# The last unit of a convolution-attention kernel: softmax in two column parities, six PSUM banks, a fused gelu, and idle matmuls

## The chip, the cores and the metric

The kernel runs on one core of one Trainium2 chip. The metric is the device time of one execution in microseconds (us); lower is better. TensorE (PE) does the matmuls and can write only to PSUM, VectorE (DVE) and ScalarE (ACT) work element by element and read PSUM and SBUF, GpSimd (POOL) adds in SBUF, SyncE (SP) issues the loads and stores.

## The reference

`x` is 4 x 256 x 64 x 64 in float32. Two layers follow each other:

```
k    = conv7x7(x, w1, dilation 2) + b1 ; k = conv1x1(k, w2) + b2      # 49 logits a pixel
attn = softmax(k, axis=1)                                             # over the 49 taps
y    = sum over taps (u,v) of attn[u,v] * x shifted by (2u, 2v)       # 256 channels
g    = gelu(yc[c, column] + y * D[c]);  o = y + g                     # yc from a small linear scan
out  = layer_norm over the 256 channels of o, times ln_w, plus ln_b
```

## The kernel before, in words

Dilation 2 lets even and odd image rows be treated apart, so the work is cut into 8 **units** (4 images x 2 row parities), each of 32 rows x 64 columns x 256 channels. Each unit passes through these stages: the convolution on PE (`conv`, into the four PSUM banks of `cv`); the logits `Z`, with a column parity `w` (even or odd columns) as an index; the softmax; the spreading of the attention into banded matrices; the application of the bands to the turned input `XT`; gelu and residual; and the layer norm. A software pipeline written out by hand, one instruction list per engine, does the convolution of unit n while the later stages of unit n-1 run on the other engines and in gaps of PE. The order of each list is the order of execution on its engine; semaphores (`wait_ge`) join the lists.

After the convolution of the last unit nothing is left to overlap with. The functions `unit(...)` end, and a tail for unit `m = 7` is written out on each engine:

- **Softmax.** PE turns the logits of one column parity into the two banks of `wk` (`turn_logits`, L457), DVE sums the taps into `E` (`gather_taps`, L1208 and L1210), and only then may PE turn the other parity into the same banks. DVE takes the maximum over the 49 taps (L1216), ACT does 16 exponentials of 128 x 49 (L737), DVE divides (L1222 to L1226), ACT rounds the result to fp16 (`attention_high`, L742), DVE makes the remainder (`attention_low`, L1230). All of these but the turning and the gathering work on both parities at once, 128 x 784 elements. PE turns the attention into `ms` (`turn_attention`, L467) and ACT copies it to `AT` (L746).
- **Spread.** Ten rows r: PE does 32 small matmuls into `wk[:, r % 2]` (`spread`, L478), ACT copies the bank to `band` in fp16 (`band_high`, L751), DVE makes the remainder (`band_low`, L1235). Row r waits for `band_low` of row r-2.
- **Application.** Eight pieces y: half of the rows q, half of the channels h, column parity w. PE does 15 matmuls into `wk[:, y % 2]` (`apply`, L495). ACT scales the bank into `o` (`attended`, L760). For each pair of column parities DVE makes the argument of gelu (`gelu_args`, L1250), ACT applies gelu (L766), DVE adds (`residual`, L1256).
- **Layer norm of the last unit in quarters.** POOL sums the halves (L408), PE makes the mean (`last_mean`, L669), DVE centres (L1571), ACT squares (L982), PE makes the variance into `cv` (`last_variance`, L677), ACT loads another table of functions (L1010) and makes the inverse deviation (L987, L989), DVE normalises (L1579), and the quarters are stored.

Unit 6 still owes parts of its own layer norm at that point: `variance` (L516), `inverse_deviation` (L781, L783), two `normalise` on DVE (L1269), two `scale_shift` on ACT (L787) and two stores behind them.

## Time and profile before

| | us |
|---|---|
| median of 3 runs | 895.67 (894.84 to 896.17) |
| profiled execution | 896.21 |
| its span | 894.4 |
| PE busy | 803.0 (90%) |
| DVE busy | 722.4 (81%) |
| ACT busy | 519.9 (58%) |
| POOL busy | 188.4 (21%) |

The span runs from the first to the last recorded event of the profiled execution. Positions below are in us from its start. "Busy" counts compute instructions only. A matmul's record is pipelined with its neighbours, so that the start of the next instruction tells more than the length of one. The granted clock of TensorE is given as a share of its 2.4 GHz level: 1.00 is 2.4 GHz and 0.50 is 1.2 GHz.

### The profile page before, as it was taken

The page shows a single profiled execution, that of the slowest core. Times are in us where ns is not written, and L with a number is a line of the kernel's source. Part 1 is how long each engine was busy: PE and PEld are TensorE (multiplying, and loading weights), DVE is VectorE, ACT ScalarE, POOL GpSimd, SP SyncE. Part 2 cuts the span into 40 slices and gives each one's busy share as a digit, 9 for nine tenths or more (in the row PEclk, how much of TensorE's full clock was granted, in tenths as well). Part 3 has the DMA queues.
Part 4 walks back from the last instruction along what each step waited for, and adds up shares of the span by engine and source line. Part 5 has one row for each costly group of instructions (what it writes and reads, how often), then busy time and mean ns, then how long its engine had stood idle before and what let it go on. Part 6 is the DMA issues. An engine that isn't in the chain of part 4 may idle for free.

```text
span 894.4 us, 27128 instructions
## 1 busy us (share of the span) xinstructions
PE 803.0 (90%) x12261; PEld 493.8 (55%) x12261; DVE 722.4 (81%) x876; ACT 519.9 (58%) x834; POOL 188.4 (21%) x100
## 2 busy tenths in 40 slices
PE   4979787999997999899997999899989999996485
PEld 4975333575555655565564645565546655663451
DVE  3899769889995999689986999599967999677336
ACT  2363232766674666665584767557665659465546
POOL 3114102112510233013311151024301341021010
PEclk9999889999997999999997999999997999999588
DMA  9322005000125010700151011601070011002103
GB/s 312 72 52 45 2 2 95 2 3 2 48 53 92 3 48 2 143 3 1 49 113 33 2 48 42 104 1 40 11 143 2 1 49 50 3 1 64 32 1 94
DMA packets 133597, 41.78 MB, mean 47 GB/s; under 512 B 133145, under 2 KB 133226, under 8 KB 133226
## 3 DMA queue, kind: packets, MB, share of 16 engines
q1 hardware_dynamic: 132248, 40.01, 19.9%
q8 instruction: 96, 1.57, 0.7%
q10 hardware_dynamic: 1234, 0.04, 0.1%
q14 instruction: 19, 0.16, 0.1%
HBM read 23.27 MB, written 16.78 MB: 45 GB/s over the span
## 4 chain that ended last, share of the span: by engine, by line
PE 51%; DVE 15%; issue 12%; ACT 11%; DMA 8%; POOL 1%; SPq 1%; DVEq 0%; ACTq 0%; POOLq 0%
PE cv L438 26%; DMA raw<-in_x_dram 7%; PE wk L495 6%; PE pcomp L603 5%; PE wk L478 4%; PE ms L516 3%; ACT chs L737 3%; ACT V L700 3%; PE wk L529 2%; DVE R L1028 2%; DVE tg L1250 2%; PE wk L457 2%; DVE V L1110 1%; DVE XT L1139 1%; DVE Z L1158 1%
## 5 line engine op out<-in xcount | busy, mean ns | idle before, releaser
L438 PE MATMUL cv<-V,W 128*32 128x496 f16 (+6 forms) x7840 | 447.1, 383 | 19.7 <-issue 7.5
L438 PEld LDWEIGHTS cv<-V,W 128*32 128x32 f16 (+1 forms) x7840 | 201.5, 97 | 224.7 <-issue 41.6
L313 POOL TENSOR_TENSOR R<-raw 128x1152 f32<-128x1152 f32 x32 | 100.2, 3130 | 258.4 <-DVE V L1110 93.8
L700 ACT ACTIVATE V<-R,sc 128x1024 f16<-128x1024 f32 (+1 forms) x88 | 110.5, 1274 | 55.1 <-PE cv L438 54.3
L1110 DVE SCALAR_TENSOR_TENSOR V<-R,sc,V 128x1024 f16<-128x1024 f32 (+1 forms) x88 | 122.4, 1399 | 9.7 <-ACT V L700 9.6
L478 PE MATMUL wk<-AT,sel 128*128 128x16 f16 x2560 | 85.1, 192 | 23.1 <-DVE band L1235 21.2
L495 PE MATMUL wk<-band,XT 128*128 128x224 f16 (+1 forms) x960 | 102.9, 268 | 2.6 <-DVE band L1235 1.4
L478 PEld LDWEIGHTS wk<-AT,sel 128*128 128x128 f16 x2560 | 79.6, 103 | 44.7 <-DVE band L1235 29.6
L495 PEld LDWEIGHTS wk<-band,XT 128*128 128x128 f16 x960 | 83.3, 99 | 25.5 <-issue 5.3
L1235 DVE TENSOR_TENSOR band<-wk,band 128x512 f16<-128x512 f32 x80 | 54.7, 689 | 44.0 <-ACT band L751 43.8
L751 ACT CAST band<-wk 128x512 f16<-128x512 f32 x80 | 46.7, 584 | 69.4 <-PE wk L478 68.4
L731 ACT ACTIVATE XT<-wk,sc 128x512 f16<-128x512 f32 x64 | 42.9, 681 | 53.6 <-PE wk L529 52.9
L760 ACT ACTIVATE o<-wk,sc 128x512 f32<-128x512 f32 x64 | 45.7, 730 | 46.7 <-PE wk L495 46.6
L1041 DVE SCALAR_TENSOR_TENSOR R<-R 128x1024 f32<-128x1024 f32 (+1 forms) x56 | 72.5, 1298 | 0.2
L1028 DVE SCALAR_TENSOR_TENSOR R<-raw 128x512 f32<-128x512 f32 (+1 forms) x48 | 48.2, 1047 | 27.5 <-DMA raw<-in_x_dram 27.4
L1139 DVE SCALAR_TENSOR_TENSOR XT<-wk,sc,XT 128x512 f16<-128x512 f32 x64 | 47.2, 746 | 16.5 <-ACT XT L731 16.3
L338 POOL TENSOR_TENSOR chs<-o 128x1024 f32<-128x1024 f32 x14 | 36.7, 2622 | 110.4 <-DVE o L1256 95.1
L344 POOL TENSOR_TENSOR chs<-tg 128x1024 f32<-128x1024 f32 x14 | 34.5, 2462 | 96.3 <-ACT tg L773 96.3
L603 PE MATMUL pcomp<-w2t,w1raw 128*128 128x48 f32 x196 | 45.0, 418 | 9.4 <-DMA w1raw<-in_L_conv_w_dram 9.4
L1250 DVE SCALAR_TENSOR_TENSOR tg<-o,dcol,yc 128x1024 f32<-128x1024 f32 x32 | 40.4, 1279 | 13.4 <-ACT o L760 13.1
L529 PEld LDWEIGHTS wk<-id,raw 128*128 128x128 f32 x256 | 35.1, 208 | 27.9 <-issue 14.2
L603 PEld LDWEIGHTS pcomp<-w2t,w1raw 128*128 128x128 f32 x196 | 43.7, 312 | 10.0 <-issue 9.6
(138 smaller groups left out, 903.1 us busy)
## 6 DMA issues: line engine op xcount, KB each, us to landing
raw<-in_x_dram SPq DMA_DIRECT2D x16, 1024.0 KB, 11.5
out_dram<-o SPq DMA_DIRECT2D x28, 512.0 KB, 3.9
w1raw<-in_L_conv_w_dram SPq DMA_DIRECT2D x2, 3136.0 KB, 16.8
out_dram<-o SPq DMA_DIRECT2D x8, 256.0 KB, 3.4
cm<-in_L_conv_Cmat_dram ACTq DMA_DIRECT2D x1, 32.0 KB, 8.4
dcol<-in_L_conv_D_dram ACTq DMA_DIRECT2D x2, 0.5 KB, 9.8
lnw<-in_L_conv_ln_w_dram ACTq DMA_DIRECT2D x2, 0.5 KB, 7.2
lnb<-in_L_conv_ln_b_dram ACTq DMA_DIRECT2D x2, 0.5 KB, 7.2
```

What stands on the lines that cost most here:

```text
L313: nc.gpsimd.tensor_tensor(R[buffer][:, :, :, :], rows_of(par, j + 2), rows_of(par, j), ALU.subtract).then_inc(pool_rows, 1)
L438: ins = pe.matmul(to.rearrange("p (w t c) -> p w t c", w=2, c=COLS)[:, :, :, c0:c1], W[:, ws, h * K7 + v, k0:k1], slot(n, a)[:, low, :, t0 ...
L478: ins = pe.matmul(wk[:, r % 2, c * TILES:(c + 1) * TILES].rearrange("p (w j) -> p w j", w=2), sel[:, s, f:f + P], AT[:, :, r:r + 29:4, c], ...
L495: ins = pe.matmul(wk[:, y % 2, (r0 - 16 * q) * COLS:(r1 - 16 * q) * COLS], XT[:, xl, 8 * w + j, h, :], band[:, bl, 8 * w + j, r0 - 4 * j + ...
L603: last = pe.matmul(pcomp[:, g % 3, v * P:v * P + REL], w1h[:, u * K7 + v, :], w2t[:, 0:REL], start=True, stop=True)
L700: nc.scalar.activation(v_array(n, a, 0), array(a), ACT.Identity, scale=sc[:, par, 3:4]).then_inc(vhi, 1)
L1028: nc.vector.scalar_tensor_tensor(out=R[buffer][:, 0:wins, h, :], in0=raw[par][:, h, r:r + 4 * wins - 3:4, :], scalar=-4.0, in1=raw[par][:, ...
L1041: nc.vector.scalar_tensor_tensor(out=part(*out), in0=part(*a), scalar=factor, in1=part(*b), op0=ALU.mult, op1=ALU.add).then_inc(row_made, 1)
L1110: nc.vector.scalar_tensor_tensor(out=v_flat(n, a, 1), in0=array_flat(a), scalar=sc[:, par, 3:4], in1=v_flat(n, a, 0), op0=ALU.mult, op1=AL ...
L1139: nc.vector.scalar_tensor_tensor(out=low, in0=wk[:, g % 2, :], scalar=sc[:, par, 3:4], in1=high, op0=ALU.mult, op1=ALU.subtract).then_inc( ...
L1235: nc.vector.tensor_tensor(band[:, 1, :, r, :], wk[:, r % 2, :].rearrange("p (c t) -> p t c", t=TILES), band[:, 0, :, r, :], ALU.subtract). ...
L1250: nc.vector.scalar_tensor_tensor(out=tg[:, h], in0=o[:, q, h], scalar=dcol[:, h:h + 1], in1=yc[:, h].unsqueeze(1).broadcast_to([P, 16, WID ...
```

## The change

Only the last unit's tail is changed, on all engines but SP.

1. **Softmax per column parity.** The logits of parity 0 are turned into `wk`, those of parity 1 into `cv[:, 0:2]`, without a wait between them. Sums, maximum, exponentials, division, rounding and turning back are done for each parity by itself (128 x 392 elements); the attention is turned into `cv` banks 2 and 3 instead of `ms`.
2. **Unit 6's remainders** move: the first `normalise` goes behind the division of parity 0, the second behind the attention's remainder of parity 1; the two `scale_shift` go between `band_high` of rows 1 and 2 and of rows 3 and 4.
3. **Idle matmuls.** `keep_running` puts 22 and then 9 matmuls of 128 x 480, whose results nobody reads, on PE into `wk` bank 0 while the softmax runs.
4. **Six banks.** `spread` and `apply` of the last unit rotate over `wk` and `cv` (6 banks) instead of `wk` alone (2). The variances of the last layer norm go to `var_bank`, all four of `cv`.
5. **Gelu and sum straight from PSUM.** `attended` is dropped. For each piece y, DVE makes the argument from PSUM (`last_args`), ACT applies gelu to 128 x 512 (`last_gelu`), and DVE reads PSUM again for the sum (`last_residual`). A column `ds` = `dcol` times the scale is made once.

The core of the diff:

```diff
+IDLE_MATMULS = (22, 9)
+        last_banks = [wk[:, 0, :], wk[:, 1, :]] + [cv[:, i, :] for i in range(4)]
+        spread_bank = lambda m, r: last_banks[r % 6] if m == LAST else wk[:, r % 2, :]
+        apply_bank = lambda m, y: last_banks[(0, 1, 4, 5, 2, 3, 0, 1)[y]] if m == LAST else wk[:, y % 2, :]
...
-                if r >= 2:
-                    pe.wait_ge(blo, 10 * m + r - 1)
+                banks = 6 if m == LAST else 2
+                if r >= banks:
+                    pe.wait_ge(blo, 10 * m + r - banks + 1)
...
+                if m == LAST and y >= 6:
+                    pe.wait_ge(l_res, y - 5)
+                if m < LAST and y >= 2:
                     pe.wait_ge(xs_made, 8 * m + y - 1)
...
+            def keep_running(w):
+                if w == 0:
+                    pe.wait_ge(l_soft, 2)
+                for _ in range(IDLE_MATMULS[w]):
+                    pe.matmul(wk[:, 0, 0:5 * 2 * REL], id16[:, :], W[:, 0, 0:5, :].rearrange("p s k -> p (s k)"),
+                              start=True, stop=True)
...
-            turn_logits(m, 0)
-            turn_logits(m, 1)
-            turn_attention(m, 0)
-            turn_attention(m, 1)
+            last_logits(0)
+            last_logits(1)
+            keep_running(0)
+            last_attention(0)
+            keep_running(1)
+            last_attention(1)
...
-            for i in range(2):
-                pool.wait_ge(o_made, 4 * (UNITS - 1) + 2)
+                pool.wait_ge(l_res, 4)
...
+            for y in range(7):
+                last_gelu(y)
             last_squares(0)
-            gelu(m, 1, 1)
+            last_gelu(7)
...
+                nc.vector.scalar_tensor_tensor(out=tg[:, h, :, w:WIDTH:2],
+                                               in0=apply_bank(m, y).rearrange("p (r c) -> p r c", c=COLS),
+                                               scalar=ds[:, h:h + 1],
+                                               in1=yc[:, h, w:WIDTH:2].unsqueeze(1).broadcast_to([P, 16, COLS]),
+                                               op0=ALU.mult, op1=ALU.add).then_inc(l_args, 1)
...
+                nc.vector.scalar_tensor_tensor(out=o[:, q, h, :, w:WIDTH:2],
+                                               in0=apply_bank(m, y).rearrange("p (r c) -> p r c", c=COLS),
+                                               scalar=scale_of_last, in1=tg[:, h, :, w:WIDTH:2],
+                                               op0=ALU.mult, op1=ALU.add).then_inc(l_res, 1)
```

How the instructions now stand. TensorE behind the last variance of unit 6, before; `wk<-id,Z` turns logits, `ms<-id,HL` turns the attention, and in the list after this one `wk<-AT,sel` is a matmul of a spread row:

```order
L457 MATMUL wk<-id,Z 128x128 [waits x_turned_low,logit_steps]
L457 MATMUL wk<-id,Z 128x128 x7
L457 MATMUL wk<-id,Z 128x128 [waits softmax_steps]
L457 MATMUL wk<-id,Z 128x128 x7
L467 MATMUL ms<-id,HL 128x128 [waits normed,softmax_steps]
L467 MATMUL ms<-id,HL 128x128 x7
```

The same place in the changed kernel:

```order
L677 MATMUL wk<-id,Z 128x128 [waits x_turned_low,logit_steps]
L677 MATMUL wk<-id,Z 128x128 x7
L677 MATMUL cv<-id,Z 128x128 x8
L686 MATMUL wk<-W,id 128x480 [waits last_softmax_steps]
L686 MATMUL wk<-W,id 128x480 x21
L692 MATMUL cv<-id,HL 128x128 [waits last_softmax_steps]
L692 MATMUL cv<-id,HL 128x128 x7
L686 MATMUL wk<-W,id 128x480 x9
L692 MATMUL cv<-id,HL 128x128 [waits last_softmax_steps]
L692 MATMUL cv<-id,HL 128x128 x7
L492 MATMUL wk<-AT,sel 128x16 [waits att_copied]
L492 MATMUL wk<-AT,sel 128x16 x63
```

The second turning has lost its wait, the turning back is in two parts, and the 22 and 9 idle matmuls stand in PE's list ahead of one part each. ScalarE over the softmax and the spread in the changed kernel (before, the two `o<-o,lnb,lnw` stood ahead of 16 exponentials in a row, one cast, two copies to `AT` and ten `band` casts):

```order
L1017 ACTIVATE chs,st<-chs,st 128x49 x3
L1022 CAST HL<-chs 128x8x49 [waits last_softmax_steps]
L1017 ACTIVATE chs,st<-chs,st 128x49 [waits last_softmax_steps]
L1017 ACTIVATE chs,st<-chs,st 128x49 x3
L1026 COPY AT<-cv 128x1024 [waits att_turned]
L1022 CAST HL<-chs 128x8x49 [waits last_softmax_steps]
L1026 COPY AT<-cv 128x1024 [waits att_turned]
L795 CAST band<-wk 128x16x32 [waits band_spread] x2
L831 ACTIVATE o<-o,lnb,lnw 128x1024 [waits normed]
L795 CAST band<-cv 128x16x32 [waits band_spread] x2
L831 ACTIVATE o<-o,lnb,lnw 128x1024 [waits normed]
```

VectorE at the end of the application in the changed kernel, where `tg<-` is `last_args`, `o<-...,tg` is `last_residual` and `o<-o,ms` is a half of a centring:

```order
L1696 SCALAR_TENSOR_TENSOR tg<-wk,ds,yc 128x512 [waits y_done,last_residual]
L1708 SCALAR_TENSOR_TENSOR o<-cv,sc,tg 128x512 [waits last_gelu]
L1673 TENSOR_TENSOR o<-o,ms 128x512 [waits last_residual,q_mean,q_sum]
L1673 TENSOR_TENSOR o<-o,ms 128x512
L1696 SCALAR_TENSOR_TENSOR tg<-wk,ds,yc 128x512 [waits y_done,last_residual]
L1708 SCALAR_TENSOR_TENSOR o<-wk,sc,tg 128x512 [waits last_gelu]
```

Each piece now has one pair of DVE instructions of 512 elements a partition; before, a pair of pieces had two of 1024, behind two copies on ACT.

## Rows read from the trace of the kernel before

**Rows 1.** The page's costly groups (count, busy us, mean ns, idle) and its DMA issues.

```profile
L751 ACT CAST band<-wk 128x512 f16<-128x512 f32 x80 | 46.7, 584 | 69.4 <-PE wk L478 68.4
...
out_dram<-o SPq DMA_DIRECT2D x28, 512.0 KB, 3.9
```

**Rows 2.** Windows of the tail: busy us (instructions) by engine, PEclk, DMA share, GB/s.

```profile
820.00:824.00 4.00, 1.89 (x16) 1.42 (x14) 3.17 (x4) 2.68 (x3) 0.00 (x0) 0.96 0.00 0
840.00:844.00 4.00, 3.12 (x98) 2.90 (x95) 2.10 (x4) 2.20 (x4) 0.00 (x0) 0.50 0.00 0
857.00:858.00 1.00, 1.00 (x8) 0.70 (x7) 0.00 (x0) 0.00 (x0) 0.00 (x0) 0.58 0.00 0
860.00:864.00 4.00, 3.21 (x35) 2.64 (x33) 1.68 (x3) 2.60 (x5) 0.00 (x0) 1.00 0.02 4
```

**Rows 3.** Timeline of TensorE: start, us, line, tiles, count [idle before, releaser].

```profile
797.08 3.36 PE L438 MATMUL cv<-V,W 128*32 128x480 f16 x60
...
822.18 1.09 PE L457 MATMUL wk<-id,Z 128*128 128x128 f32 x8 [1.38 <-DVE chs L1210]
835.63 1.89 PE L467 MATMUL ms<-id,HL 128*128 128x128 f16 x16 [12.36 <-DVE HL L1230]
838.68 2.10 PE L478 MATMUL wk<-AT,sel 128*128 128x16 f16 x64 [1.17 <-ACT AT L746]
...
852.36 8.89 PE L495 MATMUL wk<-band,XT 128*128 128x224 f16 x60 [1.40 <-DVE band L1235]
862.05 3.21 PE L495 MATMUL wk<-band,XT 128*128 128x96 f16 x30 [0.79 <-ACT o L760]
...
868.73 1.12 PE L669 MATMUL ms<-chs,ones 128*128 128x512 f32 x2 [1.37 <-POOL chs L408]
869.69 1.68 PE L495 MATMUL wk<-band,XT 128*128 128x96 f16 x15
```

**Rows 4.** Timeline of VectorE.

```profile
816.06 0.75 DVE L1139 SCALAR_TENSOR_TENSOR XT<-wk,sc,XT 128x512 f16<-128x512 f32 x1 [1.12 <-ACT XT L731]
...
820.83 0.69 DVE L1208 TENSOR_REDUCE chs<-wk 128x256 f32<-128x512 f32 x1 [1.65 <-PE wk L457]
...
822.12 2.35 DVE L1269 TENSOR_TENSOR o<-o,ms 128x1024 f32<-128x1024 f32 x2
...
825.74 0.97 DVE L1216 TENSOR_REDUCE st<-chs 128x16 f32<-128x784 f32 x1
...
832.19 0.25 DVE L1222 RECIPROCAL st<-st 128x16 f32<-128x16 f32 x1 [5.28 <-ACT chs L737]
...
832.69 0.97 DVE L1226 TENSOR_TENSOR chs<-chs,st 128x784 f32<-128x784 f32 x1
...
851.61 0.69 DVE L1235 TENSOR_TENSOR band<-wk,band 128x512 f16<-128x512 f32 x1 [0.27 <-ACT band L751]
...
873.36 1.28 DVE L1571 TENSOR_TENSOR o<-o,ms 128x512 f32<-128x512 f32 x2
```

**Rows 5.** Timeline of ScalarE.

```profile
823.38 2.37 ACT L787 ACTIVATE o<-o,lnb,lnw 128x1024 f32<-128x1024 f32 x2 [1.29 <-DVE o L1269]
...
833.70 0.86 ACT L742 CAST HL<-chs 128x784 f16<-128x784 f32 x1 [1.54 <-DVE chs L1226]
836.70 1.93 ACT L746 COPY AT<-ms 128x1024 f16<-128x1024 f16 x2 [2.14 <-PE ms L467]
...
873.48 1.06 ACT L766 ACTIVATE tg<-tg 128x1024 f32<-128x1024 f32 x1 [0.33 <-DVE tg L1250]
...
875.59 1.28 ACT L1010 ACT_TABLE_LOAD   x1
```

**Rows 6.** POOL's sums for the first means: count, ns min/median/max, first to last start.

```profile
L408 POOL TENSOR_TENSOR chs<-o x2: 1271/1802/2334, 866.3 to 868.6; 128x512 f32<-128x512 f32 x2
```

**Rows 7.** Two spread rows in the middle of the kernel: timeline, then window.

```profile
270.14 2.10 PE L478 MATMUL wk<-AT,sel 128*128 128x16 f16 x64
...
270.00:272.00 2.00, 2.00 (x66) 1.86 (x63) 1.75 (x3) 0.68 (x2) 0.00 (x0) 1.00 1.35 221
```

166 lines of the change are left out of this document (125 added, 41 removed).

## Prediction

> **What bounds the kernel now.** The profiled execution took 896.21 us for a span of 894.4 (the table above); it lies 0.54 above the median of 895.67, so I subtract from 896.21 and carry the difference to the median. The change touches only what follows the last convolution. I read first the windows of the tail, then the timeline of each engine there, each time asking whose wait ends last.
>
> In the tail no engine is full; the work is one chain through all of them. The reader is to see five milestones: the first sum of logits starts at 820.83 [rows 4]; the first spread row at 838.68, the first application at 852.36, the eighth at 869.69 [rows 3]; the last table load at 875.59 [rows 5]. Behind that load the order of instructions is as before. PE waits 12.36 us for the softmax [rows 3]. Its granted clock is 0.96 of full in 820 to 824, 0.50 in the spread and 1.00 again after 858; it came back in the window 857 to 858, some 5.5 us into the application [rows 2, 3].
>
> **Term 1, softmax, 820.83 to the spread.** Before: 17.85 us. Now, with each price from a row. An instruction on 784 elements takes 0.97 on DVE and a tiny one 0.25 [rows 4]; so 392 elements take about 0.6. ACT's cast takes 0.86 for 784 [rows 5]; I take 0.53 for half. The 16 exponentials end 5.28 after DVE begins to wait for them [rows 4], so 0.33 each.
> - Parity 0: the two sums end at 822.1 (where the next row starts), then a memset, maximum and negation of 0.9: 823.0. Eight exponentials: 825.7. Reciprocal, scale and product, 0.25 + 0.2 + 0.6: 826.75. ACT casts only behind four exponentials of parity 1 (827.0): 827.5. DVE meanwhile does one normalisation of unit 6 (2.35 / 2 = 1.2 [rows 4]) to 828.0, then the remainder: 828.55.
> - Parity 1: its sums run beside the first exponentials (to 825.2); its exponentials end at 828.85, its division at 829.9. ACT is held until 830.35 by the copy of parity 0 to `AT` (1.93 / 2 [rows 5]); cast 830.9, remainder 831.5.
> - PE turns parity 1 back in some 0.8 (16 transposes take 1.89 at 0.50 [rows 3]), and ACT copies it in 1.0: the spread starts at 833.35 instead of 838.68. **Minus 5.3.**
>
> The `scale_shift` pair of 2.37 us [rows 5], ahead of the exponentials before, leaves this path. The second turning of logits no longer waits 1.38 [rows 3].
>
> The idle matmuls are costed at nothing here. 60 convolution matmuls of 480 columns, four side by side in the array, take 3.36 [rows 3], so a full-width one takes 0.22 at 1.00. The 22 run from 822.1 to 827.0 under the softmax, with 1.5 us of cover before the turning that is queued behind them. The 9 take 2.0, from 829.4 to 831.4, with 0.1 of cover. Without cover each costs 0.22, at the lower clock 0.4.
>
> **Term 2, the spread.** Before: 13.68 us for ten rows [rows 3]. Two rows take 2.10 at 0.50 in the tail [rows 2, 3] and 2.10 at 1.00 in the middle of the kernel [rows 7]: the clock changes nothing here, and a row costs 1.05. Of the 13.68, 10.5 are matmuls; the rest is PE's wait for a free bank behind each pair of rows (it is busy 3.12 of 4 us [rows 2]) and the last evacuation. With six banks no row waits: ten rows are 10.5. The last cast and the last `band_low` (0.69 [rows 4]) follow with hand-overs: 1.4. Sum 11.9; the application starts at 845.25. ACT now also does the two `scale_shift` of 1.2 each inside the spread. It needs 0.584 for a cast [rows 1], so 5.9 for ten and 8.3 with both, of 10.5: hidden from row 6 on. If the casts could not catch up this would cost up to 2.4. The stores behind them leave 12 to 14 us later, at about 837.5 and 840. The first sum into `o` waits for them at about 852, and a store lands 3.9 us after its issue [rows 1], so they are hidden too. DVE's `ds` lies before the first `band_low`, while DVE waits. **Minus 1.8.**
>
> **Term 3, first to eighth application.** Before: 17.33 us. An application costs 1.6 at 1.00 (30 matmuls in 3.21) and about 2.95 at 0.50; the first four took 8.89 with the clock returning on the way [rows 3]. I take the same 8.89, since the spread ahead of them is again 16-column matmuls, which at 0.50 did not bring the clock back [rows 2]. The first four end at 854.15; then 855.75, 857.35, 858.95 without a wait. DVE has two instructions of 512 elements from PSUM for each piece; the nearest row is 0.75 [rows 4], less back to back, so 1.4 against PE's 1.6. ACT's gelu on half of 1024 (1.06 [rows 5]) takes 0.6 and lies between them. The load of gelu's table (as long as the other one, 1.28 [rows 5]) now follows the last cast and lies under the first application. The fourth sum stands behind the fifth argument and ends at 857.2, where before POOL could begin only at 866.3 [rows 6]. POOL's first sum took 2.33 beside a DVE instruction with two inputs in SBUF, the second 1.27 [rows 6]. Now DVE reads PSUM and one SBUF tensor, so I take 1.27 and keep 2.33 for the range. The sum is there at 858.5, before PE has finished the seventh piece; the first mean starts at 858.95 and the eighth application 0.96 later (868.73 to 869.69 before [rows 3]), at 859.9: 14.65. **Minus 2.7.** With 2.33 it is 0.6 later.
>
> **Term 4, eighth application to the table load.** Before: 5.90. Now: 1.68 matmuls [rows 3], to 861.6; argument 0.7, sum 0.7, centring of the second quarter 1.28 [rows 4], half a quarter's square 0.6, to 864.9: 5.0. What goes is ACT's copy out of PSUM. **Minus 0.9.** Behind the load the other banks for the variances free nothing: its inputs came later than the banks.
>
> Sum: 5.3 + 1.8 + 2.7 + 0.9 = 10.7. From 896.21 this gives 885.5, and against the median **885.0**.
>
> **The clock, weighed.** The trace shows the full clock lost about 824, after PE's short transposes with gaps around them, and 0.50 through a spread in which PE was busy 3.12 of 4 us [rows 2]. The Trainium skill ("TensorE: Matmul & The Clock Gate", section on why this matters) says that the clock is kept by leaving no long gaps between bursts of matmuls. By that rule the 31 idle matmuls, and a spread without waits behind them, would bring the full clock into the application; that is rival A. No row shows a spread alone at 1.00 for long, so the trace doesn't settle it; since the spread failed to raise the clock, I think it fails to hold it.
>
> **Rivals.**
> - *My forecast*, half clock at the start of the application: 885.0, or 883.5 to 887 with the clock's return a few us earlier (each us of full clock there gives 0.45) and POOL's 2.33. Chance 0.66.
> - *A: the full clock lasts through the spread.* Four applications take 6.5 instead of 8.89: 885.0 - 2.4 = 882.6. For it: PE now has no long idle time. Against: its matmuls are those that did not raise the clock before. Chance 0.18.
> - *B: the idle matmuls stand in the way.* If the clock falls during them they take 0.4 each, and the turnings behind them wait. All at 0.50: 22 end at 831.9, parity 0 is turned at 832.9, 9 more end at 836.9; turning and copy bring the spread to about 838.9. Term 1 is gone: 890.5. The 9 alone at 0.50 end at 833.4, 1.9 late: 887. For it: 0.1 us of cover at the second place. Against: 22 matmuls end to end leave PE no gap for 4.9 us. Chance 0.12, mostly near 887 to 888.
> - *C: the change does little.* If the evacuation of a bank, not its number, paced the spread and the application, terms 2 to 4 would shrink to 1 or 2 and the sum to some 6.5 (889). ACT's 0.6 and DVE's 0.69 a row against 1.05 speak against it. Chance 0.02.
> - *D, the other side: the clock does not come back.* Place: the application and the layer norm. Eight applications at 2.95 and means at double time put the table load near 875, where it was; the variances and means behind it, 11 us of matmuls at 1.00, then take up to 11 more: about 905, slower by 1%. It decides once the low clock lasts past the eighth application. Against: the same matmuls brought the clock back in 5.5 us [rows 2], and now stand closer. Chance 0.02.
>
> **Range and chances.** A reaches down to 882.3, B's likely part up to 887.5; beyond lie the rest of B, C and D, about 0.1 with the tails of the rest. Range 882.3 to 887.7. The measurement can tell about 0.2% (1.8 us) from no change. All cases but D end more than 5 us below; faster 0.96, same 0.02 (for a cost that I did not see), slower 0.02.
>
> **What the next profile would show.** First spread row near 833.3, with the idle matmuls ended before the turnings; PE without waits in ten rows; application near 845.3; POOL's sum near 857; table load near 865. Term 1 is wrong if PE's list is still busy with idle matmuls when the remainder is ready. Term 2 is wrong if rows start more than 1.05 apart. Term 3 is wrong if an argument or sum takes over 0.8, since DVE then paces the pieces, or if the granted clock is not 0.50 at the start. The whole would be wrong if unit 6's stores were late for the first sum.

## The result, and the profile after

The changed kernel takes **881.72 us** (median of 4 executions, 881.4 to 882.9) beside 895.92 for the kernel before in the same comparison (894.84 to 899.35): a ratio of **0.984, interval 0.981 to 0.987**. The forecast was 885.0, from 882.3 to 887.7. The order of events and the sign were as forecast; the gain was 13 to 14 us instead of 10.7, and the time lies 0.6 us below the range. The profiled execution took 881.4 us for a span of 879.6.

The page of the changed kernel, its totals (busy us, share of the span, instructions) and the granted clock in 40 slices:

```profile
span 879.6 us, 27207 instructions
...
PE 803.8 (91%) x12292; PEld 495.6 (56%) x12292; DVE 724.7 (82%) x892; ACT 516.0 (59%) x831; POOL 189.2 (22%) x100
...
PEclk9999889999998999999998999999997999999978
```

TensorE is busy as long as before (803.8 us with the 31 idle matmuls, 803.0 then); what went is its waiting. The timeline of TensorE in the tail, to be laid beside [rows 3]:

```profile
817.98 1.04 PE L677 MATMUL wk<-id,Z 128*128 128x128 f32 x8
818.85 1.04 PE L677 MATMUL cv<-id,Z 128*128 128x128 f32 x8
820.40 4.63 PE L686 MATMUL wk<-W,id 128*128 128x480 f16 x22 [0.51 <-DVE chs L1630]
826.58 0.62 PE L692 MATMUL cv<-id,HL 128*128 128x128 f16 x8 [1.55 <-DVE HL L1651]
827.03 1.99 PE L686 MATMUL wk<-W,id 128*128 128x480 f16 x9
829.33 0.62 PE L692 MATMUL cv<-id,HL 128*128 128x128 f16 x8 [0.31 <-DVE HL L1651]
831.06 2.12 PE L492 MATMUL wk<-AT,sel 128*128 128x16 f16 x64 [1.10 <-ACT AT L1026]
833.01 4.00 PE L492 MATMUL cv<-AT,sel 128*128 128x16 f16 x128
...
842.28 4.99 PE L511 MATMUL wk<-band,XT 128*128 128x224 f16 x30 [1.41 <-DVE band L1298]
847.11 6.23 PE L511 MATMUL cv<-band,XT 128*128 128x224 f16 x60
...
855.78 1.68 PE L511 MATMUL wk<-band,XT 128*128 128x96 f16 x15
```

Three things are to be seen. Both turnings back wait for the remainder `HL`, not for the idle matmuls ahead of them: these have ended 1.55 and 0.31 us before. The spread has no wait in it; the second pair of rows starts 1.95 behind the first (831.06 to 833.01), although the group's own length reads 2.12. And the application has no wait in it, from its first piece to the first mean. The windows of the same stretch (columns as in [rows 2]):

```profile
828.00:832.00 4.00, 2.58 (x45) 1.69 (x43) 1.84 (x3) 1.69 (x3) 0.00 (x0) 1.00 0.00 0
832.00:836.00 4.00, 4.00 (x139) 4.00 (x136) 1.94 (x3) 3.37 (x6) 0.00 (x0) 0.54 0.03 6
836.00:840.00 4.00, 4.00 (x139) 4.00 (x137) 3.01 (x6) 3.21 (x6) 0.00 (x0) 0.50 0.85 215
...
844.00:848.00 4.00, 4.00 (x32) 3.14 (x31) 1.45 (x3) 0.67 (x1) 0.00 (x0) 0.75 0.00 0
```

The clock is 1.00 up to the spread and falls some 1.3 us into it, while TensorE is busy without a pause. It is back about 3.7 us into the application (half of the window 844 to 848). The timeline of VectorE in the application, one piece after another:

```profile
848.83 0.75 DVE L1696 SCALAR_TENSOR_TENSOR tg<-cv,ds,yc 128x512 f32<-128x512 f32 x1
849.49 0.74 DVE L1708 SCALAR_TENSOR_TENSOR o<-wk,sc,tg 128x512 f32<-128x512 f32 x1
850.34 0.75 DVE L1696 SCALAR_TENSOR_TENSOR tg<-cv,ds,yc 128x512 f32<-128x512 f32 x1
```

And POOL's:

```profile
853.42 2.52 POOL L421 TENSOR_TENSOR chs<-o 128x512 f32<-128x512 f32 x2 [37.31 <-DVE o L1708]
```

At the full clock the pieces are 1.51 apart (848.83 to 850.34), and two sums on POOL take 2.52.

The four parts of the tail by their milestones, in us, from the start of the first sum of logits; "rest" is from the table load of the inverse deviation to the end of the span:

| profile | first sum at | to the spread | to the application | to its eighth piece | to the table load | rest | together |
|---|---|---|---|---|---|---|---|
| before | 820.83 | 17.85 | 13.68 | 17.33 | 5.90 | 18.8 | 73.6 |
| changed | 819.06 | 12.00 | 11.22 | 13.50 | 5.07 | 18.75 | 60.5 |
| saved | | 5.85 | 2.46 | 3.83 | 0.83 | 0.0 | 13.0 |
| forecast | | 5.3 | 1.8 | 2.7 | 0.9 | 0 | 10.7 |

"First sum at" is the end of the convolution body, whose code in both kernels is the same but for the two turnings of logits at its end.

### The profile page after: what moved, and what is told of

Its sections match the earlier page's. It is cut to its first block, busy times and chain, and to the rows that moved or that the text cites. A ratio compares the mean times of both kernels' runs of the same rounds, so it can differ in the third digit from the quotient of the medians.

```text
span 879.6 us, 27207 instructions
## 1 busy us (share of the span) xinstructions
PE 803.8 (91%) x12292; PEld 495.6 (56%) x12292; DVE 724.7 (82%) x892; ACT 516.0 (59%) x831; POOL 189.2 (22%) x100
## 3 DMA queue, kind: packets, MB, share of 16 engines
HBM read 23.27 MB, written 16.78 MB: 46 GB/s over the span
## 4 chain that ended last, share of the span: by engine, by line
PE 47%; DVE 22%; ACT 12%; DMA 9%; issue 8%; SPq 1%; POOL 1%; DVEq 0%; ACTq 0%
PE cv L451 23%; DMA raw<-in_x_dram 7%; PE pcomp L619 5%; PE wk L492 4%; PE wk L511 4%; PE ms L532 3%; ACT chs L781 3%; ACT V L744 3%; DVE R L1091 3%; PE wk L545 2%; DVE tg L1313 2%; DVE V L1173 2%; DVE Z L1221 2%; DVE R L1099 2%; DVE XT L1202 2%
## 5 line engine op out<-in xcount | busy, mean ns | idle before, releaser
L451 PEld LDWEIGHTS cv<-V,W 128*32 128x32 f16 (+1 forms) x7840 | 201.5, 97 | 221.1 <-issue 37.5
L492 PE MATMUL wk<-AT,sel 128*128 128x16 f16 x2368 | 78.9, 192 | 21.8 <-DVE band L1298 19.5
L492 PEld LDWEIGHTS wk<-AT,sel 128*128 128x128 f16 x2368 | 73.8, 102 | 42.0 <-DVE band L1298 26.5
L511 PE MATMUL wk<-band,XT 128*128 128x224 f16 (+1 forms) x900 | 95.8, 267 | 1.4 <-DVE band L1298 1.4
L511 PEld LDWEIGHTS wk<-band,XT 128*128 128x128 f16 x900 | 78.0, 99 | 22.6 <-issue 6.4
L1298 DVE TENSOR_TENSOR band<-wk,band 128x512 f16<-128x512 f32 x74 | 50.5, 689 | 36.6 <-ACT band L795 36.3
L795 ACT CAST band<-wk 128x512 f16<-128x512 f32 x74 | 43.1, 583 | 63.2 <-PE wk L492 62.1
L1104 DVE SCALAR_TENSOR_TENSOR R<-R 128x1024 f32<-128x1024 f32 (+1 forms) x56 | 70.1, 1256 | 0.2
L804 ACT ACTIVATE o<-wk,sc 128x512 f32<-128x512 f32 x56 | 40.2, 733 | 38.1 <-PE wk L511 38.0
L545 PE MATMUL wk<-id,raw 128*128 128x128 f32 x256 | 42.9, 301 | 6.7 <-DVE XT L1202 5.9
```

The source lines that it names most:

```text
L451: ins = pe.matmul(to.rearrange("p (w t c) -> p w t c", w=2, c=COLS)[:, :, :, c0:c1], W[:, ws, h * K7 + v, k0:k1], slot(n, a)[:, low, :, t0 ...
L492: ins = pe.matmul(spread_bank(m, r)[:, c * TILES:(c + 1) * TILES].rearrange("p (w j) -> p w j", w=2), sel[:, s, f:f + P], AT[:, :, r:r + 2 ...
L511: ins = pe.matmul(apply_bank(m, y)[:, (r0 - 16 * q) * COLS:(r1 - 16 * q) * COLS], XT[:, xl, 8 * w + j, h, :], band[:, bl, 8 * w + j, r0 - ...
L545: ins = pe.transpose(wk[:, g % 2, c:c + P], rows[:, w:4 * WIDTH:2], id32[:, :])
L1104: nc.vector.scalar_tensor_tensor(out=part(*out), in0=part(*a), scalar=factor, in1=part(*b), op0=ALU.mult, op1=ALU.add).then_inc(row_made, 1)
L1298: nc.vector.tensor_tensor(band[:, 1, :, r, :], spread_bank(m, r).rearrange("p (c t) -> p t c", t=TILES), band[:, 0, :, r, :], ALU.subtract ...
```

## The experiments

Every kernel below is the changed kernel with the edit shown, unless it says otherwise. The table gives each one's median, its ratio to the kernel before (95% interval), and the parts of its tail as above.

| | median | ratio | first sum at | to the spread | to the application | to the eighth | together |
|---|---|---|---|---|---|---|---|
| e1 the change again | 881.15 | 0.985 (0.983 to 0.986) | 819.40 | 12.00 | 11.09 | 13.25 | 60.2 |
| e15 before again | 895.42 | 1.000 (0.998 to 1.001) | 820.48 | 17.85 | 13.66 | 17.35 | 73.6 |
| e4 joint softmax | 887.14 | 0.991 (0.990 to 0.993) | 823.08 | 16.78 | 11.18 | 14.53 | 66.3 |
| e3 two banks, spread | 884.21 | 0.988 (0.987 to 0.990) | 818.51 | 12.00 | 13.76 | 13.86 | 63.5 |
| e5 two banks, application | 891.94 | 0.997 (0.995 to 0.999) | 825.43 | 12.00 | 11.23 | 23.36 | 70.5 |
| e6 copy kept, six banks | 886.3 | 0.991 (0.989 to 0.993) | 819.72 | 12.00 | 11.22 | 16.53 | 64.5 |
| e2 no idle matmuls | 883.47 | 0.987 (0.985 to 0.989) | 818.11 | 12.90 | 11.23 | 13.05 | 61.0 |
| e11 the same again | 883.18 | 0.987 (0.985 to 0.988) | 820.03 | 12.90 | 11.23 | 13.14 | 61.1 |
| e12 only the first 22 | 881.52 | 0.985 (0.984 to 0.987) | 818.63 | 12.42 | 11.30 | 13.04 | 60.6 |
| e7 two idle in each row | 887.05 | 0.991 (0.988 to 0.993) | 822.36 | 12.01 | 14.84 | 11.72 | 62.4 |
| e16 one idle in each row | 886.07 | 0.990 (0.989 to 0.992) | 820.14 | 12.01 | 14.50 | 13.67 | 64.0 |
| e8 three idle behind the spread | 882.1 | 0.985 (0.983 to 0.987) | 819.66 | 12.00 | 11.24 | 13.21 | 60.2 |
| e9 wide spread, far apart | 907.33 | 1.014 (1.012 to 1.016) | 820.61 | 12.01 | 35.51 | 13.39 | 84.7 |
| e10 the same in all units | 1091.26 | 1.219 (1.217 to 1.221) | | | | | |
| e13 neighbouring elements | 881.26 | 0.985 (0.984 to 0.987) | 819.80 | 12.01 | 10.07 | 14.14 | 60.1 |
| e14 neighbouring and wide | 880.42 | 0.986 (0.984 to 0.988) | 819.19 | 12.01 | 10.77 | 11.71 | 58.3 |
| e17 attention relaid | 882.07 | 0.985 (0.983 to 0.988) | 820.52 | 12.67 | 13.09 | 11.72 | 61.3 |
| e18 relaid, twice as wide in the body | **878.38** | 0.981 (0.979 to 0.984) | 816.58 | 12.68 | 11.62 | 11.71 | 59.8 |

### Both kernels again: e1, e15

> The changed kernel once more, nothing edited. Theory 1 (the tail gains 13.0 us by the two profiles, the other 1.2 to 1.8 us are chance in the convolution body, where the granted clock was lost for 44 us in one profile and 58 us in the other): the tail, from the first sum of logits to the end of the span, is again 60.5 us within 0.8, while the start of that sum lies anywhere from 819 to 821; the gain over five rounds is 13 to 14 us. Theory 2 (the change also makes the body shorter): the sum starts at 819.0 to 819.2 again and the gain is 14.5 or more.

> The kernel before once more, for a second profile of it. If the tail of the first profile was typical, 73.6 us lie between the first sum of logits and the end of the span, within 0.7, and that sum starts anywhere from 818 to 825. If instead the first profile's tail was a lucky one, it is 74.3 or more and explains why the medians differ by more than the 13.0 us of the two tails.

The parts of the tail repeat within 0.3 us in both kernels. The start of the first sum does not: over the kernels whose body is the same code it lies anywhere from 818.1 to 825.4. So the change is read from the parts of the tail, and a single median has some of the body's chance in it.

The traces show most of where this chance comes from. Up to the first sum TensorE does the same instructions in each of these profiles, but they keep it busy for 756.86 us in e2, whose first sum starts at 818.11, for 758.39 in the changed kernel's profile, for 763.63 in e4 (823.08) and for 765.58 in e5 (825.43). The stretches at a granted clock of 0.50 ahead of the first sum add up to 51, 44, 61 and 65 us. A long body is in the main one with more time at 0.50; e7 is an exception (822.36, with TensorE busy 760.00). Why the clock falls for longer in one execution than in another is not shown.

Over its eight executions in two comparisons the changed kernel's median is 881.44. The kernel before, over 53 executions in the comparisons of the experiments, has 894.98; the 895.67 from which the forecast started was a median of three, 0.7 higher.

### The softmax: e4

The functions of the kernel before stand in place of `last_logits` to `last_low`, on both parities at once, and there are no idle matmuls. Unit 6's two `normalise` lie under the exponentials, and its two `scale_shift` stay in the spread, as in the changed kernel.

```diff
-            last_logits(0)
-            last_logits(1)
-            keep_running(0)
-            last_attention(0)
-            keep_running(1)
-            last_attention(1)
+            turn_logits(m, 0)
+            turn_logits(m, 1)
+            turn_attention(m, 0)
+            turn_attention(m, 1)
```

> The changed kernel with the softmax of the last unit on both column parities at once, as before, through two banks, and no idle matmuls; unit 6's scale_shift stay in the spread and its normalisations lie under the exponentials. Theory 1: of the 5.85 us that the two profiles show between the first sum and the first spread row, 1.0 comes from unit 6's work leaving the path, so this kernel is 4.9 us slower, about 886.6. Rival (unit 6's work on the path was most of it): 2.5 us slower.

The stretch to the spread is 16.78 instead of 12.00, 4.8 longer; the spread and the application are as in the changed kernel but for a clock that came back later (14.53). This takes back the split of the softmax and the idle matmuls together. Without the idle matmuls alone the stretch is 12.90 (e2, below). So of the 5.85 us of term 1, 3.9 are the split by parity (16.78 against 12.90), 0.9 the idle matmuls, and 1.1 unit 6's work off the path (17.85 against 16.78).

### Two banks for the spread: e3

```diff
-        spread_bank = lambda m, r: last_banks[r % 6] if m == LAST else wk[:, r % 2, :]
+        spread_bank = lambda m, r: wk[:, r % 2, :]
-                banks = 6 if m == LAST else 2
+                banks = 2
```

> The changed kernel with the ten spread rows of the last unit back on two banks. Theory 1 (the wait for a bank paced the spread): from the first row to the first application 13.7 instead of 11.2 us, and up to 2.4 more because two scale_shift on ScalarE now hold up a bank; 2.4 to 4.8 us slower, 884 to 886.5. Theory C (the evacuation itself paces it): 0.5 us slower or less.

TensorE's timeline in this kernel:

```profile
833.05 2.13 PE L492 MATMUL wk<-AT,sel 128*128 128x16 f16 x64 [0.45 <-DVE band L1298]
835.62 2.09 PE L492 MATMUL wk<-AT,sel 128*128 128x16 f16 x64 [0.43 <-DVE band L1298]
838.21 2.13 PE L492 MATMUL wk<-AT,sel 128*128 128x16 f16 x64 [0.49 <-DVE band L1298]
```

A pair of rows now starts every 2.57 to 2.59 and has a wait of 0.43 to 0.49 ahead of it, against 1.95 without one: 2.5 us in all (13.76 against 11.22). Six banks are worth what term 2 measured, and rival C (the evacuation itself paces) falls. The two `scale_shift` between the casts cost nothing more even here: 13.76 is about the 13.68 of the kernel before.

### Two banks for the application, and the copy kept: e5, e6

```diff
-        apply_bank = lambda m, y: last_banks[(0, 1, 4, 5, 2, 3, 0, 1)[y]] if m == LAST else wk[:, y % 2, :]
+        apply_bank = lambda m, y: wk[:, y % 2, :]
-                if m == LAST and y >= 6:
-                    pe.wait_ge(l_res, y - 5)
+                if m == LAST and y >= 2:
+                    pe.wait_ge(l_res, y - 1)
```

> The changed kernel with the eight applications of the last unit back on the two banks of wk; argument, gelu and sum still straight from PSUM. Theory 1 (the six banks are what keeps TensorE running): a bank now comes free only behind the sum of its piece, and in VectorE's list that sum stands behind the next piece's argument, so from the third piece on each waits for an argument 0.67, a gelu or sum 0.75 and hand-overs, some 1.45: six times 1.45, 8 to 9 us slower, about 890. Rival (the fused reads did it, the banks are spare): 1 us slower or less.

Its timeline of TensorE:

```profile
855.83 1.69 PE L511 MATMUL wk<-band,XT 128*128 128x224 f16 x15 [1.51 <-DVE o L1708]
859.02 1.69 PE L511 MATMUL wk<-band,XT 128*128 128x224 f16 x15 [1.50 <-DVE o L1708]
862.22 1.69 PE L511 MATMUL wk<-band,XT 128*128 128x96 f16 x15 [1.50 <-DVE o L1708]
```

The stretch is 9.9 longer (23.36), and 10 of the 13 us of the tail are gone. (One of this kernel's ten executions took 957.24; without it the median is 891.8.) A bank is held through argument, gelu and sum, and the sum of piece y stands behind the argument of piece y+1 in VectorE's list. Reading PSUM directly and having six banks for it belong together.

e6 keeps the six banks and puts `attended` (ACT's copy out of PSUM), `gelu_args` and `residual` on 1024 elements back:

```diff
-            for y in range(7):
-                last_gelu(y)
+            attended(m, 1, 0)
+            attended(m, 1, 1)
+            gelu(m, 0, 0)
...
-            last_args(0)
-            last_args(1)
-            last_residual(0)
+            gelu_args(m, 0, 0, nxt=False)
+            gelu_args(m, 0, 1)
```

> The changed kernel with ScalarE's copy out of PSUM, gelu and sum by pairs of pieces as before, but over six banks. Theory 1: TensorE still runs without waits; POOL's first sum starts at about 855.4 instead of 853.4 in the positions of the changed kernel's profile and takes 2.3 beside VectorE, the eighth application starts 2.9 later, and the rest up to the table load is 0.8 longer: 3.7 us slower, about 885. Rival (reading PSUM twice saves most of the 4.7 us of these two stretches, the banks little): 5 us slower or more.

TensorE in this kernel:

```profile
853.87 1.68 PE L511 MATMUL wk<-band,XT 128*128 128x96 f16 x15
858.54 1.10 PE L714 MATMUL ms<-chs,ones 128*128 128x512 f32 x2 [2.99 <-POOL chs L421]
```

Its POOL:

```profile
856.07 3.55 POOL L421 TENSOR_TENSOR chs<-o 128x512 f32<-128x512 f32 x2 [39.31 <-DVE o L1328]
```

The pieces run without waits, but the first mean waits 2.99 for a sum that starts later and takes longer: two sums take 3.55 beside a VectorE instruction with both inputs in SBUF, against 2.52 in the changed kernel. Gelu and sum out of PSUM are worth 3.0 us to the eighth piece (16.53 against 13.50) and 0.85 behind it (5.92 against 5.07), 3.9 together.

### The idle matmuls: e2, e11, e12

```diff
-IDLE_MATMULS = (22, 9)
+IDLE_MATMULS = (0, 0)
```

> The changed kernel without the 22 and 9 idle matmuls. Theory 1 (they hold the clock only up to the spread, which loses it anyway): the two turnings take 0.95 us instead of 0.62 each, the application again begins at 0.50 of the clock, and the kernel is 0.3 to 1 us slower, 882 to 883. Theory A (matmuls without gaps are what brings the clock back early in the application): the first four applications take 8.9 or more instead of 8.0 and the kernel is 1.5 to 2.5 us slower. Theory B (they stand in the way of the second turning): 0.3 us faster.

> The changed kernel without idle matmuls, a second time. In e2 it was 2.3 us slower by the medians and only 0.8 in the tail of the profile. Theory 1 (worth 0.7 us for the two turnings, the rest of e2 was chance of body and clock): 0.3 to 1.3 us slower than the changed kernel, 881.8 to 883. Theory A (they bring more, about 2 us, in most executions): 883.2 or more again, and the profile shows a spread or an application that is slower at its start.

With (22, 0):

> The changed kernel with the 22 idle matmuls and without the 9. Theory 1: the 9 stood with 0.3 us of cover ahead of the second turning and the clock falls in the spread with or without them; within 0.5 us of the changed kernel, the second turning at 0.62 us or, if the clock is already down, 0.95. Theory A (each idle matmul helps to hold the clock into the spread): 0.5 to 1.5 us slower.

TensorE in e2:

```profile
825.72 1.01 PE L692 MATMUL cv<-id,HL 128*128 128x128 f16 x8 [6.77 <-DVE HL L1651]
828.87 1.03 PE L692 MATMUL cv<-id,HL 128*128 128x128 f16 x8 [2.14 <-DVE HL L1651]
```

A window of it (columns as in [rows 2]):

```profile
824.00:828.00 4.00, 1.01 (x8) 0.77 (x8) 2.52 (x5) 3.12 (x13) 0.00 (x0) 0.50 0.00 0
```

The eight turnings take 1.01 and 1.03 at 0.50 instead of 0.62 at 1.00, and the spread begins 0.9 later (12.90); the clock then comes back earlier, 2.8 to 3.0 us into the application instead of 3.7 (3.2 in e1), and 0.5 to 0.9 us of tail remain. With the 22 alone the second turning takes 1.04, and the median is that of the changed kernel: the 9 buy nothing that is measured. Eight executions without idle matmuls have a median of 883.4, eight with them 881.4. The tail shows less than half of these 1.9 us; the rest is not explained. The body's chance can make some of it (the four executions of e2 lie from 880.92 to 885.16), but that it makes all of it is not shown.

### Can the clock be kept through the spread? e7, e16, e8

`HOLD` matmuls of 128 x 480 into `ms`, read by nobody, behind each row of the last spread; 2 in e7, 1 in e16:

```diff
+                if m == LAST:
+                    if r == 0:
+                        pe.wait_ge(normed, 4 * m + 4)
+                    for _ in range(HOLD):
+                        pe.matmul(ms[:, 0, 0:5 * 2 * REL], id16[:, :], W[:, 0, 0:5, :].rearrange("p s k -> p (s k)"),
+                                  start=True, stop=True)
```

> The changed kernel with two more idle matmuls of 128 x 480 behind each of the ten spread rows. Theory 1 (the spread loses the clock because its matmuls are small; full ones between them hold it): a row takes 1.4 instead of 0.96, 4.2 us in all, the granted clock is 1.00 through the spread, and the first four applications take 6.1 instead of 8.0: 2.3 us slower. Theory 2 (the clock falls whatever stands between): rows of 1.8 us, no gain in the application: 8 us slower.

> e7 with one idle matmul behind each spread row instead of two. Theory 1 (holding the clock needs some full matmuls; two a row were enough): if one is enough, 2.0 us longer rows against about 1.9 us less in the application, within 0.7 us of the changed kernel and more even from run to run; if it is not, rows of 1.4 at 0.50 and 3 to 4 us slower.

e8 has three of them between the spread and the application instead, in the pause of 1.4 us:

> The changed kernel with three idle matmuls of 128 x 480 between the last spread row and the first application, where TensorE waits 1.4 us. Theory 1 (the clock comes back some time after full matmuls begin, so beginning 1.2 us earlier brings it back earlier in some executions): 0 to 0.9 us faster, 0.4 in the mean. Rival (they end too late and delay the first application, or the return is not moved): no difference, or 0.3 slower.

A window of e7's spread:

```profile
838.00:842.00 4.00, 4.00 (x105) 3.37 (x102) 1.72 (x4) 3.30 (x5) 0.00 (x0) 1.00 0.50 130
```

The first two pieces of its application:

```profile
849.21 3.21 PE L518 MATMUL wk<-band,XT 128*128 128x224 f16 x30 [0.99 <-DVE band L1305]
```

A window of e16, with one of them:

```profile
836.00:840.00 4.00, 4.00 (x100) 3.29 (x99) 1.97 (x3) 3.00 (x6) 0.00 (x0) 0.50 0.54 138
```

Two behind each row keep the clock at 1.00, and the first 30 matmuls of the application take 3.21 instead of 4.99. They cost 3.6 in the spread and give 1.8 back: 1.9 us of loss in the tail. The median lies 5.6 above that of the changed kernel; 3.3 of this is the late first sum of this profile (822.36), and whether that is more than the body's chance is open. One behind each row costs 3.3 and doesn't keep the clock. Three behind the spread change nothing (60.2 as in e1).

### What paces a row of the spread: e9, e10, e13, e14

A row is 32 matmuls of 16 columns whose elements lie 256 bytes apart in `AT` (two runs of eight). My theory for e9 was that the loading of the weights paces the row, so that four times the columns (each result written four times, the last writing stands, values unchanged) would cost nothing and keep the clock:

```diff
-                    ins = pe.matmul(spread_bank(m, r)[:, c * TILES:(c + 1) * TILES].rearrange("p (w j) -> p w j", w=2),
-                                    sel[:, s, f:f + P],
-                                    AT[:, :, r:r + 29:4, c], start=True, stop=True)
+                    wide = min(WIDE, COLS - c) if m >= WIDE_FROM else 1
+                    to = spread_bank(m, r)[:, c * TILES:(c + wide) * TILES]
...
+                        to = to.rearrange("p (e w j) -> p e w j", w=2, e=wide)
+                        of = AT[:, :, r:r + 29:4, c].unsqueeze(1).broadcast_to([P, wide, 2, ROWS // 4])
+                    ins = pe.matmul(to, sel[:, s, f:f + P], of, start=True, stop=True)
```

> The changed kernel, with each spread matmul of the last unit streaming its 16 columns four times over into the next 64 positions of the bank (those of later columns are overwritten by their own matmuls, so the result stands). Theory 1 (a row of 32 matmuls is paced by loading weights, 30 ns each, so wider ones cost nothing at 1.00, and they hold the clock as full idle matmuls did in e7): a row stays at 1.0 us, the granted clock is 1.00 into the application, the first four pieces take 6.1 instead of 8.0 us: 1.5 to 2 us faster than the changed kernel, about 879.7. Rival (they cost their columns, 64 instead of 16, or the clock is lost before them): rows of 1.7 us, 5 to 7 us slower.

> The same wide spread matmuls in all units, not the last alone. Theory 1 (in the body the clock is lost at waits of 2 to 5 us ahead of spread rows and comes back only late because these rows are small): after such a wait wide rows at 0.50 take 1.7 instead of 1.05 us, but the clock returns one step sooner; between 3 us faster and 2 us slower than e9, and the start of the last unit's first sum varies less than the 818 to 825 seen so far. Rival: no change of the body beyond chance.

TensorE in e9:

```profile
832.62 6.95 PE L500 MATMUL wk<-AT,sel 128*128 128x64 f16 x64 [1.10 <-ACT AT L1032]
839.41 13.74 PE L500 MATMUL cv<-AT,sel 128*128 128x64 f16 x128
```

Two windows of it:

```profile
832.00:834.00 2.00, 1.38 (x13) 1.39 (x14) 0.10 (x1) 0.56 (x1) 0.00 (x0) 1.00 0.00 0
836.00:840.00 4.00, 4.00 (x42) 4.00 (x40) 0.69 (x1) 0.98 (x2) 0.00 (x0) 0.50 0.00 0
```

The theory fell. 64 matmuls take 6.79 from start to start (832.62 to 839.41), 106 ns each. The last three of a row have only 48, 32 and 16 columns, so that the mean is 61: 1.7 ns for each column. It is the same at 1.00 (13 in 1.38) and at 0.50, where the four rows from 839.41 on take 13.58 to the next start (852.99), 106 ns again. In all units it costs 196 us more than before; the page of e10 shows 258.4 us for these matmuls, that of the changed kernel 78.9. The distance of the elements was then the suspect. e13 reads 16 neighbouring elements, e14 64 neighbouring ones, in the last unit alone. Both apply an attention that is not the right one there; the work on every engine is otherwise the same.

```diff
-                                    AT[:, :, r:r + 29:4, c], start=True, stop=True)
+                    of = AT[:, 0, r, 0:TILES] if m == LAST else AT[:, :, r:r + 29:4, c]
...
+                    ins = pe.matmul(to, sel[:, s, f:f + P], of, start=True, stop=True)
```

> The changed kernel, whose spread matmuls of the last unit read 16 neighbouring elements of AT instead of 16 that lie 256 bytes apart (the attention that is applied in the last unit is then not the right one; the amount of work is the same). Theory 3 (from e9: the time of a spread matmul is that of reading far-apart elements, 1.66 ns each at either clock, and not of loading weights): a row falls below the 0.96 us, to 0.85 or less, and the kernel is 1 us or more faster. Theory 1 (weight loading paces it): rows stay at 0.96 and the time at 881.4.

> As e13 with 64 neighbouring elements a matmul instead of 16. Theory 3: the columns now cost 27 ns at 1.00, a row takes 1 us and holds the clock, the first four applications take 6.1 us, and the kernel is 1 to 2 us faster than the changed one. Rival (wide matmuls cost 106 ns each whatever they read): 907 again.

TensorE in e13:

```profile
831.81 1.78 PE L496 MATMUL wk<-AT,sel 128*128 128x16 f16 x64 [1.10 <-ACT AT L1028]
833.44 3.59 PE L496 MATMUL cv<-AT,sel 128*128 128x16 f16 x128
```

A window of its spread:

```profile
832.00:836.00 4.00, 4.00 (x159) 4.00 (x157) 1.52 (x3) 2.96 (x5) 0.00 (x0) 0.65 0.00 0
```

TensorE in e14, spread and application:

```profile
833.05 3.83 PE L498 MATMUL cv<-AT,sel 128*128 128x64 f16 x128
836.74 1.99 PE L498 MATMUL wk<-AT,sel 128*128 128x64 f16 x64
...
841.97 3.21 PE L515 MATMUL wk<-band,XT 128*128 128x224 f16 x30 [1.40 <-DVE band L1302]
```

A window of e14's spread:

```profile
836.00:840.00 4.00, 4.00 (x146) 4.00 (x143) 3.19 (x6) 3.41 (x6) 0.00 (x0) 1.00 0.90 214
```

Sixteen near elements take 0.82 to 0.86 a row instead of 0.97 (831.81 to 833.44 for the first two), and the clock still falls (0.65 in the window). The spread is 1.15 shorter (10.07), but the clock comes back 5.0 us into the application, and 0.6 of that is lost again (14.14); the median, 881.26, is that of the changed kernel, where a gain of 1 us was expected. Sixty-four near ones take 0.92 a row (833.05 to 836.74 for four), and the granted clock stays at 1.00 through the spread and into the application, which gives 1.8 us of its 13.50 back. So in e9 it was the distance between the elements, not their number, that made a row slow.

### The attention laid out anew: e17, e18

`AT` becomes `AC`, in which the 16 elements of a matmul lie near each other; ACT's copies do the laying out, and the attention applied is the real one. In e17 the last unit reads each block four times over and the others once; in e18 the others read it twice.

```diff
-        AT = sb("AT", [P, 2, ROWS + 2 * PAD, COLS], F16)
+        AC = sb("AC", [P, COLS, 4, 2, 10], F16)
...
+                        wide = min(WIDE[m == LAST], COLS - c)
+                        to = spread_bank(m, r)[:, c * TILES:(c + wide) * TILES]
+                        of = AC[:, c, (r + 1) % 4, :, (r + 1) // 4:(r + 1) // 4 + 8]
...
+                            of = of.unsqueeze(1).broadcast_to([P, wide, 2, ROWS // 4])
...
+                nc.scalar.copy(AC[:, :, :, w, 1:9], cv16[:, 2 + w, :].rearrange("p (q a c) -> p c a q", a=4, c=COLS)
```

> A version that should beat both kernels, from e14: ScalarE writes the turned attention in an order (tile AC) in which the 8 elements that a spread matmul reads for each column parity are neighbours, in all units; in the last unit each spread matmul streams its 16 columns four times over, as in e9. All outputs are computed. Theory 3 (far-apart reads made the wide matmuls of e9 slow; near ones cost their columns at the clock): as in e14, the last spread's rows take 0.95 us at a granted clock of 1.00, which lasts into the application; its tail is 58.3 to 58.8 us and the kernel 1.5 to 2 us faster than the changed one, about 879.7. Against it: in the body ScalarE does four copies of 512 to AC a unit where it did two of 1024, 0.4 us more a unit in a stretch where PE may wait for it. Rival (the repetition itself, not the distance, made e9 slow): rows of 3.4 us and 907.

> As e17, with the spread matmuls of the body streaming their 16 columns twice over. Theory 3: at 0.50 32 near columns take 27 ns and still fit under the 30 ns of a matmul, so rows don't slow down, and where the clock was lost ahead of spread rows it comes back a little sooner: 0 to 4 us faster than e17, with the granted clock of the whole run above 0.97. Rival: the body's losses are not touched, within 1 us of e17.

TensorE at the start of the last spread, in e17 and then in e18:

```profile
833.19 3.16 PE L508 MATMUL wk<-AC,sel 128*128 128x64 f16 x64 [1.46 <-ACT AC L1042]
...
829.26 2.02 PE L508 MATMUL wk<-AC,sel 128*128 128x64 f16 x64 [1.46 <-ACT AC L1042]
```

A window of e18's last spread:

```profile
832.00:836.00 4.00, 4.00 (x121) 4.00 (x118) 2.26 (x4) 4.00 (x6) 0.00 (x0) 1.00 0.42 108
```

The first two pieces of its application:

```profile
840.88 3.21 PE L525 MATMUL wk<-band,XT 128*128 128x224 f16 x30 [1.41 <-DVE band L1314]
```

The copies on ACT take 1.38 instead of 1.01, which puts the spread 0.7 later (12.68). In e17 the clock fell 0.4 us into the last spread and came back 3.4 us later; the wide matmuls cost more meanwhile (53 ns each at 0.50, 29 at 1.00), the spread took 13.09, and nothing was won. In e18, whose last unit is the same code, it stayed at 1.00, and the tail is 0.7 shorter than that of the changed kernel. The larger part is in the body: the first sum starts at 816.58, earlier than in any kernel with the body as it was (818.1 and later). In 100 to 800 us TensorE is busy 653.97 instead of 659.85, at a granted clock of 0.98 instead of 0.97. All five executions (878.21 to 879.2) lie below all eight of the changed kernel (880.22 to 882.9). It is the fastest kernel here, some 3 us faster than the changed one. The shorter rows alone did not make it: e17 has near rows in its body too, read once, and its first sum starts at 820.52, with 58 us at 0.50 ahead of it. In e18 these are 37.5 us, the fewest of all profiles, and the whole-run clock of its five executions is 0.973 to 0.978, that of e17's 0.959 to 0.973. What separates the two is the second reading in the body; that it acts by the clock is what these numbers point to, and it rests on one comparison.

## What the forecast had right, and which step failed

**Term 1, softmax (forecast 5.3, measured 5.85).** The order of events was right, and the spread starts 0.5 earlier than forecast. The turnings back run at 1.00, 0.62 each, where 0.8 was taken, and the two remainders are ready 0.3 to 0.45 earlier, counted from the first sum. What failed is that the idle matmuls stand at nothing: without them the turnings take 1.01 to 1.04, and the stretch is 0.9 longer (e2, e11).

**Term 2, spread (1.8, measured 2.46).** The banks did what was said (e3), and the casts with both `scale_shift` caught up. The step that failed is "a row costs 1.05", from "two rows take 2.10". That is the length of a group's record, which runs on past the start of the next group. From start to start two rows are 1.95 or less, so that ten take 9.8 to the end of the last record, not 10.5; this is the whole difference. [Rows 3] had the warning in them: the two matmuls of the mean at 868.73 read 1.12, and the next group starts at 869.69, 0.96 later. I used that difference there and the group's length here.

**Term 3, application (2.7, measured 3.83).** This is the largest of the misses. The step that failed is "I take the same 8.89": the first four pieces took 7.9 from start to start, as the clock came back 3.7 us into them and not 5.5. About 0.15 of this 1.0 is again the record's length against the next start; so is the later piece at 1.6, from "30 matmuls in 3.21", which is 1.51 from start to start, though it makes only 0.1 in all, since the first mean starts 1.68 behind the seventh piece. When the clock comes back is partly chance: over the kernels whose application is that of the changed one it came back 2.7 to 5.8 us into it, and the stretch was 13.04 to 14.53. The forecast's 14.65 lies at the slow end of that, beside e4, where it was 5.8. e7 and e14 bound the other end: with the clock at 1.00 throughout the stretch is 11.7. POOL's sum cost 1.27 as taken, and e6 shows the other end, 3.55 for two. The Trainium skill ("SBUF — State Buffer", section "Who interferes with whom") says that a VectorE instruction with at most one input in SBUF doesn't contend with GpSimd, outside the modes that use both ports, and that one with two such inputs contends with a GpSimd instruction that reads SBUF; the 2.52 and 3.55 agree.

**Term 4 (0.9, measured 0.83).** Right.

The four together are 13.0 us by the profiles, 2.3 more than the sum. From the profiled 896.21 that makes 883.2; the profiled execution of the changed kernel took 881.4, since its body also ended 1.8 us earlier (819.06 against 820.83). The body's code is the same and its length varies by itself, as e1, e15 and the column "first sum at" show; so this part was no effect of the change. By medians it is the same: from the 894.98 of 53 executions to 881.44 the gain is 13.5. With the measured 13.0 the forecast's own start, 895.67, would have given 882.7, just inside the range; that the time fell outside is the mis-sized terms first, and then some bad luck with the start and the body. In the tail itself the forecast was 2.3 us short of 13.0.

**Rival A** (the full clock through the spread) did not happen. No pause was needed to lose it: the clock fell 1.3 us into the spread, 0.6 in e1, and TensorE was busy 4.00 of 4 us around it. The Trainium skill ("TensorE: Matmul & The Clock Gate", section "Why this matters for your kernels") says to leave no long gaps between bursts of matmuls; the trace does not agree that this is enough. e14's spread kept it, e13's and the changed kernel's lost it, with TensorE busy 4.00 of 4 us in all three; and the same last spread kept it in e18 and lost it for 3.4 us in e17. So more near columns helped here, in one profile each, and are no guarantee.

**Rival B** (idle matmuls in the way): no. They had 1.55 and 0.31 us of cover, and the clock was 1.00 under them. **Rival C** (evacuation paces): no, by e3. **Rival D** (the clock does not come back): no; it was back in the second piece.

**Left open:** why kernels without idle matmuls have a median 1.9 higher when their tail is only 0.5 to 0.9 longer; why e7's executions are so long; and why the clock is at 0.50 for 44 us of one body and 65 of another.

## What to carry to other kernels

Price a stretch of matmuls from the start of one group to the start of the next, never from a group's own length: a group's record runs 0.15 to 0.17 us past the next start, here 7% of two rows and 5% of two pieces. Where a chain of small steps ends a kernel and PSUM banks stand free, splitting the chain in two and giving each consumer more banks pays, and reading results straight out of PSUM pays only with banks enough to hold them. Idle matmuls are worth placing only where the cover is measured. Making the real matmuls read neighbouring elements, the same ones again, kept the clock at less cost than idle matmuls did (e14, e18), but not each time (e17), so it wants a look at the granted clock of several executions.

## What the hardware showed that was not expected

- A matmul whose 16 moving elements lie 256 bytes apart costs 30 ns (0.97 us for 32), and one with 64 such elements 106 ns in the mean of a row whose last three are narrower, both at either clock. With 16 neighbouring elements it costs 25 to 27 ns, with 64 of them 29 ns at 1.00 (e14) and 53 ns at 0.50 (e17).
- The granted clock fell from 1.00 to 0.50 under matmuls that left no pause (4.00 busy of 4 us), and stayed at 1.00 under matmuls of 64 near columns at the same rate (e14; in e17 it fell under them for 3.4 us).
- One 128 x 480 matmul behind each 32 small ones did not keep the clock, two did (one profile each).
- Two additions on POOL take 2.52 us beside VectorE instructions that read PSUM and one tensor in SBUF, and 3.55 when one with two tensors in SBUF runs beside the first.
- The same body of instructions took from 818.1 to 825.4 us, with 44 to 65 us of it at a granted clock of 0.50.
